# A decoder layer's down projection: four of eleven K tiles multiplied as integer codes and scaled after the product

## What is computed

```python
def dequant_gptq(qweight, scales, zeros, groupsize):
    ...
    return q.astype(jnp.float32) * s[g] - zp[g]      # zp = (z + 1) * s
...
gate = x2 @ Wg
up = x2 @ Wu
inter = gate * jax.nn.sigmoid(gate) * up
out = (inter @ Wd).astype(jnp.float16)
...
x = _layernorm(x + _L0_ffn_ref(x, ...), axis=-1)
```

## Time and profile before

| | us |
|---|---|
| median of 3 runs | 929.53 (928.93 to 930.1) |
| profiled execution | 927.45 |
| its span | 925.70 |
| PE busy | 875.0 (95%) |
| DVE busy | 714.7 (77%) |
| POOL busy | 491.5 (53%) |
| ACT busy | 474.5 (51%) |
| first matmul of the down projection | 862.14 |
| first and last `yh` | 869.46 and 919.32 |

### The profile page before, as it was taken

One profiled execution on the slowest core, in us unless ns is written; L12 is line 12 of the kernel. 1 busy time (PEld: TensorE's weight loads), 2 busy tenths in 40 slices (PEclk: granted clock), 3 DMA queues, 4 the chain that ended last, 5 costly groups with the idle time before them and its releaser, 6 DMA issues.

```text
span 925.7 us, 17387 instructions
## 1 busy us (share of the span) xinstructions
PE 875.0 (95%) x6285; PEld 485.5 (52%) x6285; DVE 714.7 (77%) x1098; ACT 474.5 (51%) x1448; POOL 491.5 (53%) x430
## 2 busy tenths in 40 slices
PE   8888999899799999999999999999998899999997
PEld 3665776555445555555555555545545344444443
DVE  5688887887677888698797897997997556997333
ACT  4777878553455555565565555645555612333000
POOL 1264349536556676578567656768887411221011
PEclk9999999999999999999999999999999999999999
DMA  6754243330135412315244142135333120320001
GB/s 177 230 182 152 70 127 116 103 115 1 24 86 131 104 35 70 103 35 148 35 82 102 35 125 58 27 77 99 70 90 86 35 63 14 134 59 1 12 35 45
DMA packets 119174, 76.22 MB, mean 82 GB/s; under 512 B 72654, under 2 KB 103345, under 8 KB 119089
## 3 DMA queue, kind: packets, MB, share of 16 engines
q1 hardware_dynamic: 116784, 74.45, 30.4%
q10 hardware_dynamic: 2304, 0.66, 0.3%
HBM read 51.96 MB, written 6.36 MB: 63 GB/s over the span
## 4 chain that ended last, share of the span: by engine, by line
PE 55%; DVE 14%; ACT 9%; POOL 9%; issue 9%; DMA 3%; SPq 0%; ACTq 0%; DVEq 0%; POOLq 0%
PE bank L311 17%; PE bank L313 17%; PE bank L312 17%; ACT prob L692 3%; POOL rot L569 3%; DVE nmax L940 2%; POOL pn L586 2%; DVE rsin L1019 2%; DVE pT L909 2%; ACT prob L834 1%; POOL q2l L575 1%; POOL deq L593 1%; ACT pT L643 1%; DMA pT<-pn 1%; PE bank L1447 1%
## 5 line engine op out<-in xcount | busy, mean ns | idle before, releaser
L579 POOL TENSOR_TENSOR prob<-prob,rden 128x512 f32<-128x512 f32 x64 | 66.5, 1040 | 129.3 <-DVE rden L1084 129.3
L569 POOL TENSOR_TENSOR rot<-rcos,rsin 128x512 f32<-128x512 f32 x80 | 106.5, 1331 | 30.6 <-DVE rsin L1019 30.5
L311 PE MATMUL bank<-aTh,xqh 128*128 128x512 f16 x256 | 98.2, 384 | 6.3 <-DVE aTl L909 4.5
L312 PE MATMUL bank<-aTl,xqh 128*128 128x512 f16 x256 | 98.3, 384 | 0.0
L313 PE MATMUL bank<-aTh,xql 128*128 128x512 f16 x256 | 98.2, 384 | 0.0
L311 PE MATMUL bank<-xoh,o2h 128*128 128x512 f16 x256 | 97.8, 382 | 0.1
L312 PE MATMUL bank<-xol,o2h 128*128 128x512 f16 x256 | 97.7, 381 | 0.0
L313 PE MATMUL bank<-xoh,o2l 128*128 128x512 f16 x256 | 97.7, 381 | 0.0
L834 ACT ACTIVATE prob<-bank,ebias 128x128 f32<-128x128 f32 x256 | 90.6, 366 | 2.1
L1019 DVE SCALAR_TENSOR_TENSOR rsin<-bank,sinq 64x512 f32<-64x512 f32 x128 | 88.1, 688 | 1.7
L643 ACT ACTIVATE ebias<-nmax 128x4 f32<-128x4 f32 x128 | 26.9, 210 | 115.9 <-DVE nmax L1079 75.3
(11 more groups left out here) (182 smaller groups left out, 2538.4 us busy)
## 6 DMA issues: line engine op xcount, KB each, us to landing
tst<-tables SPq DMA_DIRECT2D x11, 768.0 KB, 5.9
xqs<-in_xwq SPq DMA_DIRECT2D x8, 1024.0 KB, 5.6
xos<-in_xwo SPq DMA_DIRECT2D x8, 1024.0 KB, 5.5
qst<-in_fq SPq DMA_DIRECT2D x11, 384.0 KB, 3.5
kstk<-stack SPq DMA_DIRECT2D x48, 64.0 KB, 2.3
qstk<-stack SPq DMA_DIRECT2D x21, 128.0 KB, 2.6
xs<-in_ctxT SPq DMA_DIRECT2D x2, 1024.0 KB, 7.2
res<-in_x SPq DMA_DIRECT2D x1, 2048.0 KB, 8.4
```

Source lines behind the costliest of these rows:

```text
L311: pe.matmul(out_ap, ah, bh, start=first, stop=False)
L312: pe.matmul(out_ap, ah, bl, start=False, stop=False)
L569: nc.gpsimd.tensor_tensor(rot[:, r % 2, :], rcos[:, r % 2, :], rsin[:, r % 2, :], ALU.add).then_inc(rope_rot, 1)
L579: nc.gpsimd.tensor_tensor(prob[:, v % 2, :].rearrange("p (h k) -> p h k", h=QH), prob[:, v % 2, :].rearrange("p (h k) -> p h k", h=QH), rd ...
```

## The change

The last four K tiles of the down projection (7 to 10) are multiplied as codes. What VectorE leaves for them is code minus zero, a small integer that f16 holds exactly (`wdc`), so there is no rest and two products do for three. Each of the four has a bank of its own (`part_bank`, six banks in turn), because its scale varies by column and can only be applied after the product: VectorE multiplies the bank by the scale row (`scale_part`, into `part`, f32), and GpSimd adds the four parts in two pairs and one sum (`add_parts`). `add_ffn` adds that sum to the bank of the other seven tiles, which now has two banks in turn (6 and 7). The scale rows (`wds`) are loaded to all partitions in four more DMAs. For these tiles `dif` and `deq` cover gate and up only, and `wdh` and `wdl` are gone.

```diff
+DOWN_CODES = (7, 8, 9, 10)
+DOWN_SPLIT = tuple(i for i in range(NI) if i not in DOWN_CODES)
...
+                if i in DOWN_CODES:
+                    sp.wait_ge(c_wo, STEPS)
+                    sp.dma_start(wds[i][:, :], tables_d[1, 3 * i + 2, :].partition_broadcast(P)).then_inc(scales_in, 16)
...
-                    pool.wait_ge(f_dlo, i - 1)
-                nc.gpsimd.tensor_tensor(deq[:, i % 2, :], dif[:, i % 2, :], tst[:, i % 2, 1, :], ALU.mult).then_inc(f_deq, 1)
+                    pool.wait_ge(f_dlo, split_before(i - 1))
+                w = (2 if i in DOWN_CODES else 3) * D
+                nc.gpsimd.tensor_tensor(deq[:, i % 2, 0:w], dif[:, i % 2, 0:w], tst[:, i % 2, 1, 0:w], ALU.mult).then_inc(f_deq, 1)
+
+            def add_parts(b):
+                pairs = len(DOWN_CODES) // 2
+                for p in range(pairs):
+                    pool.wait_ge(f_part, len(DOWN_CODES) * b + 2 * p + 2)
+                    nc.gpsimd.tensor_tensor(part[:, 2 * p, :], part[:, 2 * p, :], part[:, 2 * p + 1, :],
+                                            ALU.add).then_inc(f_pair, 1)
+                pool.wait_ge(f_pair, pairs * (b + 1))
+                nc.gpsimd.tensor_tensor(part[:, 0, :], part[:, 0, :], part[:, 2, :], ALU.add).then_inc(f_parts, 1)
...
             for b in range(NB):
+                add_parts(b)
                 inverse_sd(2 * NB + b)
...
-                nc.vector.tensor_tensor(dif[:, i % 2, :], nib[:, :], tst[:, i % 2, 0, :], ALU.subtract).then_inc(f_dif, 1)
+                w = (2 if i in DOWN_CODES else 3) * D
+                nc.vector.tensor_tensor(dif[:, i % 2, 0:w], nib[:, 0:w], tst[:, i % 2, 0, 0:w], ALU.subtract).then_inc(f_dif, 1)
+                if i in DOWN_CODES:
+                    nc.vector.tensor_tensor(wdc[i][:, :], nib[:, 2 * D:], tst[:, i % 2, 0, 2 * D:], ALU.subtract).then_inc(f_dcode, 1)
...
+            def scale_part(b, e):
+                use = len(DOWN_CODES) * b + e
+                dve.wait_ge(f_yc, use + 1)
+                if use == 0:
+                    dve.wait_ge(scales_in, 16 * len(DOWN_CODES))
+                nc.vector.scalar_tensor_tensor(out=part[:, e, :], in0=part_bank(use)[:, :], scalar=2.0 ** (-E_I - E_W),
+                                               in1=wds[DOWN_CODES[e]][:, :], op0=ALU.mult, op1=ALU.mult).then_inc(f_part, 1)
+
             def add_ffn(b):
                 dve.wait_ge(f_y, b + 1)
-                nc.vector.tensor_scalar(yh[:, b % 2, :], bank[4 + b % 4][:, :], 2.0 ** (-E_I - E_W), None,
-                                        ALU.mult).then_inc(f_y16, 1)
+                dve.wait_ge(f_parts, b + 1)
+                nc.vector.scalar_tensor_tensor(out=yh[:, b % 2, :], in0=bank[6 + b % 2][:, :], scalar=2.0 ** (-E_I - E_W),
+                                               in1=part[:, 0, :], op0=ALU.mult, op1=ALU.add).then_inc(f_y16, 1)
...
+            for e in range(len(DOWN_CODES)):
+                scale_part(0, e)
             for b in range(NB):
                 add_ffn(b)
                 statistics(2, b)
+                if b + 1 < NB:
+                    for e in range(len(DOWN_CODES)):
+                        scale_part(b + 1, e)
                 normalised(2, b)
...
+            def down_codes(b):
...
+                for e, k in enumerate(DOWN_CODES):
+                    use = len(DOWN_CODES) * b + e
+                    if use in (2, 4):
+                        pe.wait_ge(f_inter, len(GATE_UP) - 2 + use // 2)
+                    if use >= 6:
+                        pe.wait_ge(f_part, use - 5)
+                    dst, ti = part_bank(use)[:, :], slice(b * S, (b + 1) * S)
+                    pe_.matmul(dst, inh[k][:, ti], wdc[k][:, :], start=True, stop=False)
+                    pe_.matmul(dst, inl[k][:, ti], wdc[k][:, :], start=False, stop=True).then_inc(f_yc, 1)
+
             def down(b):
...
-                if b >= 4:
-                    pe.wait_ge(f_y16, b - 3)
-                for k in range(NI):
+                if b >= 2:
+                    pe.wait_ge(f_y16, b - 1)
+                for k in DOWN_SPLIT:
...
             for b in range(NB):
+                down_codes(b)
                 down(b)
```

More of the change, by code:

```diff
@@ L260, in decoder_kernel @@
         wd_at = (67, 77.5, 159.5, 87.5, 89.5, 91.5, 93.5, 95.5, 97.5, 107.5, 109.5)
-        wdh = [at(kb, f"wdh{i}", [P, D], F16) for i, kb in enumerate(wd_at)]
-        wdl = [at(kb + 1, f"wdl{i}", [P, D], F16) for i, kb in enumerate(wd_at)]
+        wdh = {i: at(wd_at[i], f"wdh{i}", [P, D], F16) for i in DOWN_SPLIT}
+        wdl = {i: at(wd_at[i] + 1, f"wdl{i}", [P, D], F16) for i in DOWN_SPLIT}
+        wdc = {i: at(wd_at[i], f"wdc{i}", [P, D], F16) for i in DOWN_CODES}
+        wds = {i: at(wd_at[i] + 1, f"wds{i}", [P, D], F16) for i in DOWN_CODES}
+        part = at(42, "part", [P, len(DOWN_CODES), D], F32)
         in_at = (115.5, 119.5, 123.5, 127.5, 131.5, 135.5, 139.5, 143.5, 147.5, 151.5, 0)
@@ L332, in turn_bank, with part_bank, split_before @@
             return bank[4 + 3 * (u % 2)]
+        def part_bank(use):
+            return bank[(use + 4) % 6]
+        def split_before(i):
+            return sum(1 for k in DOWN_SPLIT if k < i)
         def by_k(tile):
@@ L415, in load_codes @@
                     sp.wait_ge(f_deq, i - 1)
+                if i - 2 in DOWN_CODES:
+                    sp.wait_ge(f_dcode, DOWN_CODES.index(i - 2) + 1)
                 sp.dma_start(qst[:, i % 2, :].rearrange("p (m n) -> p m n", m=3),
@@ L863, in weights_hi @@
                                      ACT.Copy).then_inc(f_whi, 1)
-                nc.scalar.activation(wdh[i][:, :], deq[:, i % 2, 2 * D:], ACT.Copy).then_inc(f_whi, 1)
+                if i in DOWN_SPLIT:
+                    nc.scalar.activation(wdh[i][:, :], deq[:, i % 2, 2 * D:], ACT.Copy).then_inc(f_whi, 1)
             def gate_sigmoid(n):
@@ L1125, in codes @@
                     dve.wait_ge(f_deq, i - 1)
-                nc.vector.tensor_tensor(dif[:, i % 2, :], nib[:, :], tst[:, i % 2, 0, :], ALU.subtract).then_inc(f_dif, 1)
+                w = (2 if i in DOWN_CODES else 3) * D
+                nc.vector.tensor_tensor(dif[:, i % 2, 0:w], nib[:, 0:w], tst[:, i % 2, 0, 0:w], ALU.subtract).then_inc(f_dif, 1)
+                if i in DOWN_CODES:
+                    nc.vector.tensor_tensor(wdc[i][:, :], nib[:, 2 * D:], tst[:, i % 2, 0, 2 * D:], ALU.subtract).then_inc(f_dcode, 1)
             def weights_lo(i):
-                dve.wait_ge(f_whi, 2 * i + 1)
+                dve.wait_ge(f_whi, i + split_before(i) + 1)
                 nc.vector.tensor_tensor(wgl[i % 4][:, :, :].rearrange("p m n -> p (m n)"), deq[:, i % 2, 0:2 * D],
                                         wgh[i % 4][:, :, :].rearrange("p m n -> p (m n)"), ALU.subtract).then_inc(f_wlo, 1)
-                dve.wait_ge(f_whi, 2 * i + 2)
-                nc.vector.tensor_tensor(wdl[i][:, :], deq[:, i % 2, 2 * D:], wdh[i][:, :], ALU.subtract).then_inc(f_dlo, 1)
+                if i in DOWN_SPLIT:
+                    dve.wait_ge(f_whi, i + split_before(i) + 2)
+                    nc.vector.tensor_tensor(wdl[i][:, :], deq[:, i % 2, 2 * D:], wdh[i][:, :], ALU.subtract).then_inc(f_dlo, 1)
             def gate_times_up(n):
@@ L1493, in gate_up @@
                             [wgl[i % 4][:, m, k * P:(k + 1) * P] for k in range(NK)], aTh, aTl, cols).then_inc(done, 1)
+            def down_codes(b):
+                if b % BH == 0:
+                    pe.wait_ge(f_ilo, GU_POS[(NI - 1, b // BH)] + 1)
+                if b == 0:
+                    pe.wait_ge(f_dcode, len(DOWN_CODES))
+                    pe.wait_ge(late_lo, BH)
+                for e, k in enumerate(DOWN_CODES):
[7 more added lines that the diff above has]
+                    pe_.matmul(dst, inl[k][:, ti], wdc[k][:, :], start=False, stop=True).then_inc(f_yc, 1)
             def down(b):
-                pe.wait_ge(f_ilo, GU_POS[(NI - 1, b // BH)] + 1)
                 if b == 0:
-                    pe.wait_ge(f_dlo, NI)
-                    pe.wait_ge(late_lo, BH)
-                if b >= 4:
-                    pe.wait_ge(f_y16, b - 3)
-                for k in range(NI):
-                    last = split_products(pe_, bank[4 + b % 4][:, :], inh[k][:, b * S:(b + 1) * S], inl[k][:, b * S:(b + 1) * S],
-                                          wdh[k][:, :], wdl[k][:, :], k == 0, k == NI - 1)
+                    pe.wait_ge(f_dlo, len(DOWN_SPLIT))
+                if b >= 2:
+                    pe.wait_ge(f_y16, b - 1)
+                for k in DOWN_SPLIT:
+                    last = split_products(pe_, bank[6 + b % 2][:, :], inh[k][:, b * S:(b + 1) * S], inl[k][:, b * S:(b + 1) * S],
+                                          wdh[k][:, :], wdl[k][:, :], k == DOWN_SPLIT[0], k == DOWN_SPLIT[-1])
                 last.then_inc(f_y, 1)
```

2 lines of the change are left out of this document (added).

## The result

The changed kernel takes 933.38 us (median of 20 runs, 931.26 to 936.22) against 929.63 us for the kernel before (20 runs, 928.58 to 932.11): ratio 1.0038, 95% interval 1.003 to 1.0046. It is slower by 0.4%, and the forecast was 933.0 us. The profiled execution has a span of 930.1 us.

A forecast was written before the change was run, and what follows sets the result against it. TensorE bounds the down projection before, a VectorE-GpSimd loop after: `yh` of batch 0 at 868.66 plus seven turns (54.11) gives 922.77 against 919.32; 3.45 added to the median 929.53 gives 933.0 us, range 930.7 to 936.0.

The forecast's parts named there:

- The loop: Down projection: `yh`, statistics, four scalings, three additions, next `yh` take 7.73 us a turn, against 6.26 us of matmuls.
- GpSimd's addition: Down projection: adding one 128x512 f32 part to another on GpSimd takes 1.27 us, like `rot`.
- Rival 3: Down projection: GpSimd's additions take 1.04 us like `prob`, loop 7.29 us, no change at 929.2 us; chance 0.08.
- The seam: Between GpSimd's two pair additions VectorE's `res<-res,lnmv,lnrs` slips in and costs GpSimd 0.17 us.
- Rival 1: Between the pair additions `res` holds GpSimd for all its 0.55 us; loop 8.11 us, 935.7 us; chance 0.22.
- rival 2: Between the pair additions `res` costs GpSimd nothing; loop 7.56 us, 931.8 us; part of the forecast's range.
- The first `yh`: Down projection, batch 0: `yh` starts at T + 7.54 = 868.66, T = 861.12 being the first down matmul's start.
- Gate and up: Gate and up stage: VectorE's savings make TensorE the bound and gain exactly 1.02 us; `wgl` shrinks to about 3 us.
- The tail: Behind the last batch of the down projection: 6.38 us without a matmul, untouched since no scalings follow.
- The sum: Whole kernel: last `yh` at 922.77 against 919.32, a shift of 3.45 us added to the median, 933.0 us.
- Rival 4: Down projection: loop hidden behind matmuls, turn under 6.26 us or scalings ahead of `yh`; 7.9 us sooner, 921.6; chance 0.05.
- Rival 5: Down projection: TensorE's idling lowers its clock; at half clock the kernel takes some 35 us more; chance 0.01.

The follow-up runs named there:

- two code tiles: Changed kernel's order with two code tiles (9 and 10) instead of four, so two scalings and one addition per batch; 925.7 us, ratio 0.9962 to the kernel before.
- scalings ahead: Changed kernel reordered: `part` in two buffers, VectorE scales batch b+1 before `yh` of batch b; 922.55 us, ratio 0.9936 to the kernel before.
- three products again: Changed kernel with three matmuls again for the code tiles, 33 instead of 29 per batch; 933.73 us, ratio 1.0048 to the kernel before.
- additions on VectorE: Changed kernel with the three additions per batch on VectorE instead of GpSimd; 928.07 us, ratio 0.998 to the kernel before.
- no additions: Changed kernel without GpSimd's additions, `yh` adding the first part alone, output incomplete; 920.54 us, ratio 0.9911 to the kernel before.
- the tail mended: Version with VectorE's scalings of b+1 before `yh` of b, norm of batch 6 moved behind the statistics of batch 7; 922.02 us, ratio 0.9925 to kernel before.

## Why the prediction was right, and where it was not

- **The loop**, the term that counts seven times: 7.73 forecast, 7.75 measured. By its parts, from the start of `yh`: scalings from 2.28 (forecast 2.28); GpSimd's first pair from 3.62 (3.67); second pair done at 6.31 (6.34); last addition done at 7.66 (7.70); next `yh` at 7.76 (7.73). The scalings step by (2.45 - 0.69) / 3 = 0.59 us, nearer to the 0.60 of the earlier trace rows than to the 0.70 that I kept for the range, and the handover from GpSimd to VectorE took 0.10 instead of 0.03 us. These two errors nearly cancel, which is luck, though of some 0.05 us a turn only.
- **GpSimd's addition** is priced like `rot` in the earlier trace rows, 1.27 us, not like `prob`. Rival 3 falls.
- **The seam.** The two pairs take 2.50 us in batch 0, where no `res<-res,lnmv,lnrs` stands beside them, and 2.69 in the others: 0.19 us, against 0.17 taken from the earlier trace rows. Rival 1 (0.55) and rival 2 (nothing) both fall. But the prediction took 0.17 for a price of its own, at odds with a full hold, and there it was wrong. In the changed kernel the second addition starts at 874.36, finds `res` in progress until 874.70 and ends at 875.82, 1.12 us behind the end of `res`. The same holds wherever an addition meets a VectorE instruction on SBUF tiles alone (the scalings and `yh`, which read a bank, delayed none): an overlap of 0.34 us makes it 1.46 us long, one of 0.38 us (two code tiles) 1.50, one of 0.47 us (`res<-res,yh`, scalings ahead) 1.60, and each time it ends 1.12 to 1.13 us behind VectorE's instruction. So GpSimd is held until `res` ends; it costs only 0.20 us because `res`, 0.54 us long, had started 0.20 us ahead of the addition, and because 0.14 us of the addition's own 1.26 pass during the hold. The rule of the Trainium skill ("SBUF — State Buffer", "Who interferes with whom"), that the one that comes second is blocked until the first has finished, agrees with these times. What rival 1 had wrong is the length of the hold: it let `res` begin its 0.55 us at the end of GpSimd's first addition (874.40), and `res` ended 0.30 us behind that. That the 0.17 carried over is luck in part: the overlap was 0.31 us in the earlier trace rows and 0.34 here.
- **The first `yh`**: T + 7.57 against T + 7.54.
- **Gate and up.** From a `nib` ahead of the changed tiles to the first down matmul it was 862.14 - 789.92 = 72.22 us, and is now 861.94 - 790.74 = 71.20: 1.02 us less, as forecast. The same stretch takes 71.20 to 71.21 us in the six other versions with four code tiles, three products again left aside. But one step of this term was wrong: "`wgl` should shrink from 4.11 to about 3 us". It shrank to 1.21, and `inl`, ahead of it, grew from 0.68 to 2.61 us:

```profile
822.63 0.42 DVE L1160 TENSOR_TENSOR wdc<-nib,tst 128x512 f16<-128x512 uint16 x1
822.97 2.61 DVE L1186 TENSOR_TENSOR inl<-gated,inh 128x512 f16<-128x512 f32 x1
825.50 1.21 DVE L1164 TENSOR_TENSOR wgl<-deq,wgh 128x1024 f16<-128x1024 f32 x1
...
822.80 2.24 POOL L613 TENSOR_TENSOR deq<-dif,tst 128x1024 f32<-128x1024 f16 x1 [7.70 <-DVE dif L1158]
```

  The new `wdc` is in progress when `deq` asks; `deq` comes next, and the instruction behind `wdc` is held. The sum of the two is about the same (3.82 us, against the 3.7 forecast), and nobody waits for `inl` here, so the error cost nothing; had a matmul waited for it, it could have. I also put weight on the shorter `deq`, where the dropped `wdl` would have done without it.
- **The tail** is unchanged, as forecast: its 6.31 us against 6.38 go by spans rounded to a tenth; by 925.66 and 930.12 us it is 6.34 before and 6.33 after.
- **The sum.** From the first down matmul to the last `yh` the stage grew by 4.67 us (61.85 against 57.18), less 1.02 us ahead of it, less 0.01 in the tail: 3.64 us, against 3.45 forecast. The spans differ by 4.46, of which 0.82 is there before the first changed instruction takes effect and is not the change's (at the same `nib` the trace of the scalings ahead is 0.65 us sooner than that of before, that of the additions on VectorE 2.23 later); the medians differ by 3.75.
- **Rival 3's sum** has a slip: with additions of 1.04 us the first `yh` would come 0.47 us sooner, not 0.67, since the second pair waits for the fourth scaling (T + 4.78 + 0.09 + 1.04 + 0.09 + 1.04 + 0.03 = T + 7.07). That is 929.4 instead of 929.2, and changes nothing.
- **Rival 4** named its own condition rightly: under 6.26 us a turn, or scalings that run ahead of `yh`. Both were tried (no additions, scalings ahead), and both ended at TensorE's bound, 50.27 and (with the tail mended) 50.29 us from the first down matmul to the last `yh`; 231 x 0.2158 + 0.42 = 50.27 had been worked out for it.
- **Rival 5**, the clock: it was granted 1.00 from the first `yh` to 916.04 us, through gaps of TensorE of up to 1.16 us, so the matmuls kept their step. It was lower only where hardly a matmul was left: 0.73 in the last turn, with five of them, and 0.50 in the tail.

## What to carry to other kernels

When work is handed from one engine to another and back within one iteration, and the next iteration's share is queued behind the answer, add up the round trip and compare it with the bound of the stage; the busy shares (here 66% for VectorE and 61% for GpSimd in the slowed stage) say nothing about it. If the round trip is too long, put the first half of the next iteration ahead of the second half of this one and give the buffer between them a second copy, before counting what the change saves elsewhere. In a closed loop even a busier engine can be the better place for a step than a slower idle one.

## What the runs showed of the hardware beyond that

- Which VectorE instruction is held by GpSimd depends on who is there first, and small instructions decide it: with 0.42 us of `wdc` inserted, a wait of 1.9 us (of 2.9 with `deq` at full length) lay on `inl` and no longer on `wgl`. A held instruction with two inputs ended 0.55 us behind GpSimd's (`inl`, 825.58 against 825.03), although it takes 0.69 by itself.
- A VectorE addition of two SBUF tiles that meets GpSimd's additions lengthens both: `res<-res,yh` from 0.69 to 1.04 and GpSimd's last addition from 1.27 to 1.60 us, in batches 2 to 7 of the eight in the version with the scalings ahead (in batch 1 `res<-res,yh` takes 1.29).
- TensorE's granted clock was 0.96 over the seven turns, but its gaps of 1.15 us in each 7.75 did not lower it. By stretches of the changed kernel's trace (columns as in the earlier trace rows):

```profile
869.51:916.04 46.53, 43.05 (x195) 18.27 (x194) 30.51 (x54) 0.00 (x0) 28.44 (x30) 1.00 0.09 34
916.04:923.79 7.75, 0.97 (x5) 0.24 (x3) 5.08 (x10) 0.00 (x0) 4.74 (x5) 0.73 0.09 34
```

  The lower clock falls where TensorE has run out of matmuls, 0.73 there and 0.50 in the tail, where the kernel before had 0.84; so it cost nothing.
